# A 1-core macaron kernel (routed FFN, long convolution, routed FFN): the routing of the first half of the tokens rewritten, and GpSimd's queue put in another order

## The reference

```
x = x + 0.5 * ffn(layernorm(x))
x = x + attn(layernorm(x))       # gate, long convolution over time, layernorm, gated MLP, projection
x = x + 0.5 * ffn(layernorm(x))

def ffn(x):                       # 12 experts, the best 3 for each token
    logits = x @ Wg
    topw, sel = top_k(logits, 3);  topw = softmax(topw)
    y = gelu(x @ Wup[e] + bup[e]) @ Wdown[e] + bdown[e]     # 128 -> 512 -> 128, for the chosen e
    return sum over the 3 chosen e of topw * y
```

## Time and profile before

| | |
|---|---|
| time of 3 runs | 706.76, 709.73, 709.92 us, median 709.73 |
| time of the profiled execution | 706.28 us, its span 704.5 us |
| PE busy | 574.6 us (82%), 4616 instructions |
| DVE busy | 364.0 us (52%) |
| ACT busy | 408.2 us (58%) |
| POOL busy | 428.4 us (61%), 433 instructions |
| first `up` of phases 0, 1 and 3 | 66.18, 209.22 and 540.33 us |

### The profile page before, as it was taken

The page is one execution under the profiler, slowest core; times in us unless marked ns, Lnnn a source line. Parts: engine busy times, 40 slices in busy tenths (PEclk is TensorE's granted clock), DMA queues, the critical chain, the costliest instruction groups (busy, mean ns, idle before and its releaser), DMA issues. The chain is left out here.

```text
span 704.5 us, 18117 instructions
## 1 busy us (share of the span) xinstructions
PE 574.6 (82%) x4616; PEld 529.8 (75%) x4616; DVE 364.0 (52%) x1675; ACT 408.2 (58%) x1235; POOL 428.4 (61%) x433
## 2 busy tenths in 40 slices
PE   2323999887889889899996999989998999899650
PEld 2313999877889877788996988778987999889510
DVE  6792455342113699976650789987561322322134
ACT  2101766664456677777673778777664666556340
POOL 1326677777737775076765777045774676676773
PEclk9999999999999999999997999999999999999965
DMA  9604666767678665455587866346667877766193
GB/s 255 179 1 129 190 197 196 197 161 223 158 208 249 182 204 159 132 145 168 171 248 207 245 203 190 96 142 180 190 194 214 259 208 227 198 197 184 35 242 97
DMA packets 127559, 127.90 MB, mean 182 GB/s; under 512 B 17258, under 2 KB 90785, under 8 KB 127461
## 3 DMA queue, kind: packets, MB, share of 16 engines
q1 hardware_dynamic: 111684, 99.26, 49.1%
q0 software_dynamic: 12992, 26.11, 13.1%
q10 hardware_dynamic: 2784, 1.38, 0.7%
HBM read 96.62 MB, written 30.79 MB: 181 GB/s over the span
## 5 line engine op out<-in xcount | busy, mean ns | idle before, releaser
L826 ACT ACTIVATE hT<-ps,BU 128x128 f32<-128x128 f32 x944 | 268.3, 369 | 136.2 <-PE ps L698 133.5
L698 PE MATMUL ps<-xT,WU 128*128 128x128 f32 x1888 | 257.3, 281 | 7.2 <-ACT hT L826 3.1
L709 PE MATMUL ps<-WD,hT 128*128 x1888 | 252.1, 277 | 13.6 <-DVE Ys L1203 13.3
L698 PEld LDWEIGHTS ps<-xT,WU 128*128 128x128 f32 x1888 | 236.7, 196 | 18.7 <-issue 17.4
L709 PEld LDWEIGHTS ps<-WD,hT 128*128 128x128 f32 x1888 | 230.7, 193 | 17.8 <-issue 17.5
L533 POOL DMA_INDIRECT xs<-XN,SX x144 | 146.3, 1016 | 105.6 <-issue 72.1
L546 POOL DMA_INDIRECT YG<-ys,SY x144 | 151.0, 1049 | 68.7 <-issue 39.9
L1203 DVE TENSOR_TENSOR Ys<-ps,BD 128x128 f32<-128x128 f32 x236 | 67.1, 288 | 219.1 <-PE ps L709 211.2
L899 DVE SCALAR_TENSOR_TENSOR X<-YG,WK,X 128x128 f32<-128x128 f32 x144 | 50.8, 352 | 60.9 <-DMA YG<-ys,SY 56.7
L520 POOL DMA_INDIRECT xl<-xn,SG x59 | 60.5, 1026 | 33.8 <-issue 17.2
L555 POOL DMA_INDIRECT yk<-Ys,row x59 | 58.6, 993 | 31.1 <-issue 14.1
(11 more groups left out here) (200 smaller groups left out, 495.6 us busy)
## 6 DMA issues: line engine op xcount, KB each, us to landing
WU<-in_L_ffn_Wup_dram SPq DMA_DIRECT2D x236, 256.0 KB
ys<-Ys SPq DMA_DIRECT2D x39, 256.0 KB, 2.8
xl<-xs SPq DMA_DIRECT2D x118, 66.0 KB
xl<-xs SPq DMA_DIRECT2D x59, 64.0 KB
WD<-in_L_ffn_Wdown_dram SPq DMA_DIRECT2D x12, 256.0 KB, 5.4
WD<-yk SPq DMA_DIRECT2D x12, 256.0 KB, 5.3
xs<-XN,SX POOLq DMA_INDIRECT x144
YG<-ys,SY POOLq DMA_INDIRECT x144, 3.4
```

The lines of the kernel that those rows point to most:

```text
L698: x = e.matmul(HB[i % 2][:, c * P:(c + 1) * P], WU[i % NW][:, c * P:(c + 1) * P], xT[m % 2][:, j * P:(j + 1) * P], start=True, stop=True)
L709: x = e.matmul(YB[i % 2][:, 0:D], hT[i % 3][:, c * P:(c + 1) * P], WDf[:, bass.ds(r + c * P, P)], start=(c == 0), stop=(c == C - 1))
L826: x = e.activation(hT[i % 3][:, c * P:(c + 1) * P], HB[i % 2][:, c * P:(c + 1) * P], ACT.Gelu, bias=BU[:, bass.ds(b + c, 1)])
```

## The change

1. TensorE gets `warm(26)` ahead of the first routing step, `warm(20)` behind the last `L` and `warm(16)` behind `I`: transposes of the identity into a PSUM bank that nobody reads.
2. The tile one-hots are compared for four blocks at a time (`TE`, 12 x 59 = 708 values in each instruction), and ScalarE multiplies them by the token's number into `TO` (16 steps `TO`). The constants `iop` and `iotp` become float16.
3. GpSimd works out the table for the first 4 tiles alone (`s_tf`), with which SP loads the first `WU`; VectorE makes the rest of it behind `SG`. The bias work moves to tile 3 (VectorE) and tile 5 (SP) of phase 0.
4. The first group is turned, copied and waited for tile by tile (`turn_first`); group 1 is turned behind tile 3 and not behind tile 0.
5. GpSimd's queue: in phase 0 `SCATTERED` sets how many scatters are issued by gather k (none before gather 24, then 3 for every 5 gathers); in phase 3 `FETCHED` grows by 13/25 for each tile and not by 2/5, and a block is combined 8 tiles behind its last fetch and not 3.

```diff
 FIRST = [("A", "N", 3), ("PA", "T", 0), ...
-         ("P", "L", 2), ("P", "L", 3), ("P", "KB", 0), ("A", "Z", 0), ("P", "I", 0)]
+         ("P", "L", 2), ("P", "L", 3), ("P", "KB", 0), ("A", "Z", 0), ("A", "TO", 0), ("A", "TO", 1), ("A", "TO", 2),
+         ("A", "TO", 3), ("P", "I", 0)]
+
+BIAS = [("V", "B3", 3), ("S", "B3", 5)]
...
-SCATTER_FROM = 7
+SCATTERED = tuple(max(0, (3 * (k - 10)) // 5) for k in range(NTL - AHEAD))
...
-FETCHED = tuple(min(K * NT, 6 + (2 * k) // 5) for k in range(NTL))
-FINAL_AT = tuple(next((k + 3 for k in range(NTL - 3) if FETCHED[k] >= K * (t + 1)), NTL) for t in range(NT))
+FETCHED = tuple(min(K * NT, 6 + (13 * k) // 25) for k in range(NTL))
+FINAL_AT = tuple(next((k + 8 for k in range(NTL - 8) if FETCHED[k] >= K * (t + 1)), NTL) for t in range(NT))
...
-            for k in range(NTL):
-                if k + AHEAD < NTL:
-                    gather_x(k + AHEAD)
-                while done < K * NT and (k == NTL - 1 or done <= k - SCATTER_FROM):
+            for k in range(NTL - AHEAD):
+                gather_x(k + AHEAD)
+                while done < SCATTERED[k]:
                     scatter_x(1, done // (4 * K), 0, done % (4 * K))
                     done += 1
+            while done < K * NT:
+                scatter_x(1, done // (4 * K), 0, done % (4 * K))
+                done += 1
...
-                for t in range(NT):
-                    for k in range(K):
-                        e.tensor_scalar(PO[:, t, k, :], iop[:], PF[:, t, k:k + 1], None, ALU.is_equal)
-                        i = e.tensor_scalar(TO[:, t, k, :], iotp[:], TF[:, t, k:k + 1], tok[:, t:t + 1], ALU.is_equal, ALU.mult)
-                    i.then_inc(s_oh, 1)
+                for q in range(NQ):
+                    e.tensor_tensor(
+                        TE[:, 4 * q:4 * q + 4].rearrange("p t k i -> p (t k) i"),
+                        iotp[:, :].rearrange("p (o i) -> p o i", o=1).to_broadcast([P, 4 * K, NTL]),
+                        TF[:, 4 * q:4 * q + 4].rearrange("p t k -> p (t k)").rearrange("p (n o) -> p n o", o=1).to_broadcast(
+                            [P, 4 * K, NTL]), ALU.is_equal).then_inc(s_ot, 1)
+                    for t in range(4 * q, 4 * q + 4):
+                        for k in range(K):
+                            i = e.tensor_scalar(PO[:, t, k, :], iop[:], PF[:, t, k:k + 1], None, ALU.is_equal)
+                        i.then_inc(s_oh, 1)
...
+            def turn_first(j):
+
+                ps = bank(("X", 0, 0, 0), j)
+                e.wait_ge(s_x0[j], 16)
+                e.transpose(ps[:, 0:P], xl[0][:, j, 0:D], ident[:]).then_inc(s_xp0 if j < 3 else s_xp, 1)
...
+            def warm(count):
+
+                for _ in range(count):
+                    e.transpose(HB[0][:, 0:P], ident[:], ident[:])
...
+            warm(26)
             for step in SLOTS["P"][-1]:
                 side(step)
-            turn_x(0)
-            e.wait_ge(s_b3, 48)
+                if step[0] == "L" and step[2] == NQ - 1:
+                    warm(20)
+            warm(16)
...
+                elif kind == "TO":
+
+                    e.wait_ge(s_ot, q + 1)
+                    for t in range(4 * q, 4 * q + 4):
+                        e.activation(TO[:, t].rearrange("p k i -> p (k i)"), TE[:, t].rearrange("p k i -> p (k i)"), ACT.Copy,
+                                     scale=tok[:, t:t + 1]).then_inc(s_to, 1)
```

More of the change, by code:

```diff
@@ L87, in schedule @@
         put(engines, -1, kind, 0, q, 0)
+    for engines, kind, at in BIAS:
+        put(engines, at, kind, 0, 0, 0)
     for q in range(NQ):
@@ L118, in next_group @@
     n, _, k = TILES[i]
+    if i in (0, 3):
+        return 1 if i else None
     if k % 4 == 0 and k // 4 + 1 < NG:
@@ L144, in ring @@
         if i == -1:
-            take(("X", 0, 0, 0), 1)
+            take(("X", 0, 0, 0), 4)
     return used, last
@@ L369, in _ @@
                 e.dma_start(xs[h][E * CAP:ROWS, :], pad[:, 0:DX[h]]).then_inc(s_pad[h], 16)
-            for n in range(3):
-                e.wait_ge(s_bp, 2 * n + 1)
-                e.dma_start(BO3[n:n + 1, :], bob[n][:]).then_inc(s_b3, 16)
             def load_w(i):
                 n, h, k = TILES[i]
-                if k % 4 == 0:
+                if i == 0:
+                    e.wait_ge(s_tf, 1)
+                    for j, v in enumerate(table(e, eF, 0, D * (E - 1))):
+                        w_at[j] = v
+                elif k % 4 == 0:
                     e.wait_ge(*tables_of(n))
@@ L411, in pads, with bias3 @@
                     e.dma_start(xs[h][bass.ds(pad_at[2 * (x % 2) + j], P), :], pad[:, 0:DX[h]]).then_inc(s_pad[h], 16)
+            def bias3():
+                for n in range(3):
+                    e.wait_ge(s_bp, 2 * n + 1)
+                    e.dma_start(BO3[n:n + 1, :], bob[n][:]).then_inc(s_b3, 16)
             def store_y(m):
@@ L428, in _ @@
                 for step in SLOTS["S"][i]:
-                    pads(*step[1:])
+                    if step[0] == "B3":
+                        bias3()
+                    else:
+                        pads(*step[1:])
                 for q in range(2):
@@ L688, in turn_x @@
                     wd_at[(m, j)] = v
+            def turn_first(j):
+                ps = bank(("X", 0, 0, 0), j)
+                e.wait_ge(s_x0[j], 16)
+                e.transpose(ps[:, 0:P], xl[0][:, j, 0:D], ident[:]).then_inc(s_xp0 if j < 3 else s_xp, 1)
+                if j == 0:
+                    e.wait_ge(*tables_of(0))
+                    for x, v in enumerate(table(e, eW[0], 0, HID * (E - 1))):
+                        wd_at[(0, x)] = v
+            def warm(count):
+                for _ in range(count):
+                    e.transpose(HB[0][:, 0:P], ident[:], ident[:])
             def up(i):
@@ L724, in _ @@
             for i in range(NI):
+                if i < 4:
+                    turn_first(i)
                 up(i)
@@ L833, in _ @@
                 side(step)
-            turn_x(0)
+            e.wait_ge(*tables_of(0))
+            for j, v in enumerate(table(e, eB[0], 0, C * (E - 1))):
+                b_at[(0, j)] = v
             e.wait_ge(s_bu, 1)
+            turn_first(0)
             for i in range(NI):
+                if i < 3:
+                    turn_first(i + 1)
                 gelu(i)
@@ L1163, in first @@
                 e.tensor_copy(SG[:], psum[USED[("I", 0, 0, 0)][0][0]][:, 0:NTL]).then_inc(s_sg, 1)
+                dv.on(e.tensor_tensor(
+                    ge[0:1], iotl[0:1, :].rearrange("p (i o) -> p i o", o=1).to_broadcast([1, NTL, E]),
+                    end[0:1, 0:E].rearrange("p (o e) -> p o e", o=1).to_broadcast([1, NTL, E]), ALU.is_ge))
+                e.wait_ge(s_dv, dv.n)
+                dv.on(e.tensor_reduce(EFp[:], ge[0:1], AX.X, ALU.add))
+                e.wait_ge(s_dv, dv.n)
+                dv.on(e.tensor_scalar(eip[:], EFp[:], float(E - 1), None, ALU.min))
+                e.wait_ge(s_dv, dv.n)
+                e.tensor_scalar(eB[0][:], eip[:], float(C), None, ALU.mult)
+                e.tensor_scalar(eD[0][:], eip[:], float(D), None, ALU.mult)
+                e.tensor_scalar(eW[0][:], eip[:], float(HID), None, ALU.mult).then_inc(s_tab0, 1)
                 weights(0)
```

76 lines of the change are left out of this document (43 added, 33 removed).

## The result

The changed kernel takes 670.61 us in the median of 4 runs (669.91 to 671.78), the kernel before 709.83 (706.76 to 712.69): a ratio of 0.945, 95% interval 0.941 to 0.949. I had predicted 684, from 678 to 692. The sign was right and the size wrong: the saving is 39 us, not 26.

What follows compares the result with a forecast made beforehand. GpSimd's queue was taken to bound phase 0 and the step into phase 1, with VectorE's routing ahead. Terms sum to -24.2 us on 706.28, giving 682.1, or 685.5 with 3.4 added for the median; predicted 684, range 678 to 692.

Steps and rivals of the forecast that it cites:

- One-hots: VectorE's routing: building the one-hots falls from 19.5 to 11.4 us, 8.1 us saved.
- Shorter table on GpSimd: Routing: GpSimd's first operations shrink from 708 values to 48 beside VectorE's work, 1.2 us saved (0.8 to 2).
- TensorE kept busy: Routing: transposes in TensorE's waits gain at most 3.5 us or lose 1.8; taken as 0.
- The rival at 0.15: Routing: transposes lift TensorE's clock and it holds through the routing, 3.5 us less, 680; chance 0.15.
- First group by tile: Start of phase 0: TensorE's first tile starts some 4 us earlier, but GpSimd ends the phase, so nothing counted.
- GpSimd's queue, phase 0: Phase 0: 25 gathers go first, so the first scatter no longer finds slot numbers late; 3.5 us saved.
- a sign of being wrong: Expected profile: GpSimd waiting for turns in phase 0 would show the prediction wrong; no size given.
- The clock at the step: Step into phase 1: one TensorE wait of about 13 us lets the clock fall, 2.4 us lost.
- Phase 1's start: Phase 1: `gather_y` starts some 6 us ahead of the first `up`, sparing VectorE and TensorE waits; 2.3 us saved (0 to 4).
- Phase 3: Phase 3 to the end: GpSimd no longer waits for tiles, 12 gathers left instead of 19; 11.5 us saved.
- The `yk` loads: End of phase 3: these loads are late next, ending at 141.3 us; rival that they hold the end: 690, chance 0.12.
- the clock's gain: Routing: transposes lift TensorE's clock, at most 3.5 us gained; used in the range's lower end.

Runs made afterwards that it cites:

- a run of its own: Changed kernel with the first group's four turns and copies done before the first up-projection, not tile by tile: 671.58 us, ratio 0.948 to the kernel before.
- the run with the clock kept up: Changed kernel with 56 and 28 transposes added in the waits at the steps into phases 1 and 2: 672.45 us, ratio 0.948 to the kernel before.

## Why the prediction was too high

The span's saving was 34.5 us, the sum of terms 24.2. By the prediction's own steps:

- **One-hots** (-8.1): 7.3. A `PO` cost 0.16 us as taken (12 in 29.93 to 31.88); what the old ones cost was taken too high, as 1.2 of their 19.5 us belong to the next step.
- **Shorter table on GpSimd** (-1.2, up to 2): **mis-sized**, 3.4. The casts were right, at 0.8; the three `tk` multiplications, "some more", were 1.3. From the `tk` multiplication to the one-hots it was 4.84 us before and 2.66 after (2.2 saved), and 1.2 more lay in the first ten pairs. I had taken the pairs for undisturbed.
- **TensorE kept busy** (0): **this step failed.** I set a gain of 3.5 against a loss of 1.8 and took nothing between. The clock rose, as the shorter matmuls show. It gave 3.3 us at the `tk` multiplication (29.77 to 26.46); the run without transposes lost 3.5 at the first gather, and they gave 3.2 in the kernel before. The rival at 0.15 came nearest, though the level didn't hold to the end of the routing (granted 0.53 from 24 to 30 us, when the gating matmuls were done), and fell sooner still in the kernel before with transposes. The counter-evidence to it was that TensorE, recorded as busy from 13 to 23 us, had not risen before; without the transposes it doesn't rise there now either, and with them it does. The Trainium skill ("TensorE: Matmul & The Clock Gate", Part 4: PE-mode transpose) says that transposes don't count as activity for the clock. Here 26 float32 transposes, with nothing else on TensorE beside them, brought 16 gating matmuls from 3.43 to 1.91 us: the measurement decides.
- **First group by tile** (0): right, by a run of its own.
- **GpSimd's queue, phase 0** (-3.5): 3.4 to the first `up` (2.6 to the last scatter, 0.7 from there to the turn). Right in cause for the 2.6: the wait for slot numbers is gone, less 0.9 us in the two longer steps, one of them the wait for a turn that was named as a sign of being wrong. That the sum came out at 3.4 is in part luck, by the 0.7. TensorE's end of the phase was 6.5 us later than worked out, 4.8 of it by the `WU` waits.
- **The clock at the step** (+2.4): too dear. Eight `up` cost 0.9 us more, and the run with the clock kept up gained nothing: its second turn waits for rows until 193.28 us, where the slow matmuls of the changed kernel end at 193.87.
- **Phase 1's start** (-2.3, up to 4): **mis-sized.** This is the largest miss. Phase 1 saved 4.9 us, the slow restart included, where these two steps together gave a loss of 0.1. I priced the early gathers by TensorE's waits for VectorE in 35 us; they go on, and are 4.9 us in 51, of which 0.6 is left. Both runs that made `gather_y` late again lost 5.1 and 8.1 us in phase 1 and nothing of note behind it.
- **Phase 3** (-11.5): 13.0 from the first `up`, 11.9 from the first gather (154.2 - 142.3). The size was near, the reason not, so that is luck: I took the last combine for the kernel's end. The `yk` loads were late for it (8.75 and 0.82 us of waits), it ended 149.5 us behind the first gather and not 147.0, and so saved 9, not 11.5. The span saved 11.9, since it hangs on GpSimd's last DMA. And the larger part came from `FINAL_AT` (7.0 us, measured with the old fetches), to which I gave half a sentence: "The combines come 8 tiles behind and don't wait." Of the 7 gathers moved forward, priced at some 9 us of the last gather's 14, at most 2.9 is to be seen, and 3.1 of the phase stays without a cause.

Against the terms the span thus saved 10.3 us more: clock 3.3, contention 2.2, one-hots -0.8, phase 0 -0.1, phase 1 5.0, phase 3 1.5, phase 2 -0.8. The change's median lies 1.2 us below its profile, where I had added 3.4. My range reached to 678 only, because I let its lower end be the clock's gain and phase 3 alone; that phase 1 could give more than 4 us, or GpSimd's contention more than 2, was not in it. Two slips in the working change nothing: before the last scatter of phase 3 stood 29 gathers and not 30 (the 87 distances are right), and from 11.5 to 14 it is 2.5 us, not 2.8.

## What to carry to other kernels

Where an in-order engine consumes another queue's transfers, ask what stands behind the consumer: gathers started 8.5 us earlier against the consumer were worth some 5 us here, and gathers consumed 5 tiles later 7, more than the waits for them in the first few tiles. Before an engine's last instruction is taken for the end of a program, its distance to the end of the span should be looked at, and that of the others.

## What was not expected of the hardware

- The span ends 10.0 to 10.3 us behind the start of GpSimd's last indirect DMA in all 14 traces, while the distance from the last combine goes from 2.7 to 9.9. What GpSimd does in these 10 us the profile doesn't show, and it stays open.
- 26 float32 transposes in a row bring TensorE's matmuls to the durations of 2.4 GHz: 16 gating matmuls then take 1.91 us, and 3.43 without. In the kernel before the level fell again at 17 to 19 us, and the same 16 took 2.77. 56 transposes fill a wait of 7 us, with a granted clock of 1.00 in it and eight `up` of 1.13 us behind it.
- GpSimd's operations on one partition (1x708 values) lengthen a cast of VectorE beside them from 0.19 to 0.64 us, three multiplications of 192 values each from 0.92 to 2.26, and a 59-value one-hot from 0.31 to 0.78. A 48-value subtraction and the 708-value compare are not lengthened (0.21 and 0.90 us).
